# Second layer of a four-layer kernel: value products of both batches of a pair together, in one PSUM bank, every second step

## The chip, the cores and the metric

One core of a Trainium2 chip. The metric is device time in microseconds (us) of one execution of the whole program; lower is better. Engines: TensorE (PE in the profile; PEld is its weight load), VectorE (DVE), ScalarE (ACT), GpSimd (POOL) and SyncE (SP), each with its own instruction queue, in order, tied to the others by semaphores alone.

## The reference, cut to what matters

Four layers follow one another on an array of 16 batches, 128 x 256 each. The change is in the second (L1), an attention with 16 heads of 64 over 256 positions of each batch:

```python
w_heads = Wqkv @ z + Winj @ u              # one pair of weights per half of the positions
q, k, v = split(w_heads)                   # 16 heads x 64 x 256 positions each
score = einsum('bndi,bndj->bnij', q + r_w_bias, k) * SCALE
prob = softmax(score, axis=-1)
attn_vec = einsum('bnij,bndj->bndi', prob, v)
x = Wo @ attn_vec + bo + z
return (x - mean(x)) * rsqrt(var(x) + 1e-5)   # over the 128 channels
```

## The kernel before

Layer 1 works in R1 = 8 rounds of NB = 2 batches (the first and last written out, the six between them one hardware loop, function `rounds`). A round has STEPS = 16 steps: step t takes a pair of heads, t // 2, of batch b = t % 2. All work of a step is written by hand, engine by engine, in the four functions `body`; every engine runs its own list in that order and waits at semaphores.

What a step is made of, with the lines of the profile:

- scores (L1249): q times k of two heads, each on half the rows of the array, in one score bank per head. q and k are kept as a high and a low part in fp32r, three products for one. They wait for the exponentials of the step before.
- maxima of both heads (DVE, L1430), then four exponentials with their sums (ACT, L1355), a reciprocal of the sums for each head (DVE, L1436), and the normalisation in place (GpSimd, L1195).
- turn (L1261): the probabilities of step t - L_T = t - 1, transposed by TensorE into two banks; copied to pT by ACT (head 0, L1364) and DVE (head 1, L1441), `copy_turned`.
- times_v (L1277): pT times the values, step t - L_V = t - 2, into half of bank 4, each head in 64 columns of the array. `round_heads` (ACT, L1370) takes the result's high part to aT, `rest_heads` (DVE, L1446) the low part, both 256 wide; the next times_v waits for that low part (`aT_lo`), since there is one bank.
- times_wo (L1286), in even steps: output projection of the pair t - L_W = t - 4, both batches in one product of 512, summed over the round in bank 7.
- fills, after all that: one to three units from the table FILLS. A unit q, k or v is a projection of 12 products (6 for each half of its 512 columns; L1231 for q and k, L1235 for v, in the order of the table) into one of two work banks, taken by the names' position in turn; `Banks.free` makes a unit wait until the unit two before it has been read out. A q or k is read out by ACT (high part, `round_work`, L1375, L1378) and then DVE (low part, `rest_work`, L1457, L1461); a v by DVE alone (L1452). mean (L1293), var (L1300) and inv0, inv1 (L1308) are the layer normalisation of the round before: DVE centres and squares (L1487, L1489), GpSimd raises to -1/2 (`inverse_std`, L1200), DVE makes a diagonal (`make_diagonal`, L1499, in step T_DIAG), and takes the output (L1507). A name with + belongs to the next round.

At T_ZU = 13 ACT rounds the next round's inputs z and u (`round_z`, `round_u`, L1384, L1389) and DVE takes their rest (`rest_z`, `rest_u`, L1467, L1472); SP then loads the next u. These inputs are used by every projection, so round_z first waits for the last of the round:

```python
act.wait_ge(*work.full("v3b1", i - 1))     # called with i + 1
```

In DVE's body, rest_z and rest_u stand ahead of the read-out of that step's fills. The order by hand, before:

```python
L_T, L_V, L_W = 1, 2, 4
FILLS = [("q1", "k1"), ("v0b1", "q2"), ("k2",), ("v1b0", "q3"), ("k3", "v1b1"), ("q4", "mean"), ("k4",),
         ("v2b0", "q5", "var"), ("k5",), ("v2b1", "q6"), ("k6", "v3b0"), ("q7", "k7"), ("v3b1", "inv0"),
         ("inv1",), ("q0+", "k0+"), ("v0b0+",)]
T_Y, T_CENTRE, T_READ, T_DIAG, T_ZU = 2, 6, 8, 9, 13
```

PE's body: scores(t), times_v(t-2), turn(t-1), times_wo in even steps, fills. ACT's: exponentials, copy_turned, round_heads, (z, u), round_work. DVE's: maxima, copy_turned, both reciprocals, rest_heads, residual or z and u or the diagonal where due, fills.

Of the kernel before, what the change touches and what calls it, by code (L numbers as in the profile page):

```python
# [9 lines left out]
F32 = mybir.dt.float32  # L10
# [1034 lines left out]
def layer1(nc, v):  # L1045
# [10 lines left out]
    L_T, L_V, L_W = 1, 2, 4  # L1056
    SCALE = HD1 ** -0.5
    with ExitStack() as ctx:
        def sb(name, shape, dt=F32):
            return ctx.enter_context(nc.sbuf_tensor(name, shape, dt))  # L1060
# [11 lines left out]
        def place(name, shape):  # L1072

            with nc.sbuf_tensor(name + "_raw", shape, F32) as raw:
# [14 lines left out]
        pT = sb("pT", [P, 2, BANK])  # L1089
# [11 lines left out]
        pv_bank = psum[:, 4, 0:D]  # L1101
# [13 lines left out]
        FILLS = [("q1", "k1"), ("v0b1", "q2"), ("k2",), ("v1b0", "q3"), ("k3", "v1b1"), ("q4", "mean"), ("k4",),  # L1115
                 ("v2b0", "q5", "var"), ("k5",), ("v2b1", "q6"), ("k6", "v3b0"), ("q7", "k7"), ("v3b1", "inv0"),
                 ("inv1",), ("q0+", "k0+"), ("v0b0+",)]
        T_Y, T_CENTRE, T_READ, T_DIAG, T_ZU = 2, 6, 8, 9, 13
# [14 lines left out]
        pv_done = event("pv_done", STEPS)  # L1133
        aT_hi = event("aT_hi", STEPS)
        aT_lo = event("aT_lo", STEPS)
# [81 lines left out]
        def _(pe):  # L1217
# [48 lines left out]
            def times_v(i, t):  # L1266

                pair, b = divmod(t, NB)
                if t % 4 < 2:
                    pe.wait_ge(*work.out(f"v{pair // 2}b{b}", i))  # L1270
                for h in range(2):
                    pe.wait_ge(*copied[h].at(i, t))
                pe.wait_ge(*aT_lo.at(i, t - 1))
                for kt in range(2):
                    for h in range(2):
                        at = (2 * (pair % 2) + h) * HD1
                        last = mm(pv_bank[h * HD1:(h + 1) * HD1, :], vs[:, pair // 2 % 2, b, kt, at:at + HD1],  # L1277
                                  pT[:, h, kt * D:(kt + 1) * D], start=kt == 0, stop=kt == 1)
                last.then_inc(pv_done.sem, 1)

            def times_wo(i, pair):
                pe.wait_ge(*aT_lo.at(i, NB * pair + NB - 1))
# [29 lines left out]
            def body(i, first, last):  # L1312
                for t in range(STEPS):
                    scores(i, t)
                    if t >= L_V or not first:
                        times_v(i, t - L_V)
                    if t >= L_T or not first:
                        turn(i, t - L_T)
                    if first and t == L_W:
                        pe.wait_ge(wo_lo_made, 1)  # L1320
                    if t % 2 == 0 and (t >= L_W or not first):
                        times_wo(i, (t - L_W) // 2) if t >= L_W else times_wo(i - 1, (t - L_W) // 2 + PAIRS)
                    for name, r in fills(i, t, last):
# [26 lines left out]
        def _(act):  # L1350
# [10 lines left out]
            def copy_turned(i, t):  # L1361
                act.wait_ge(*turned.at(i, 2 * t))
                act.wait_ge(*pv_done.at(i, t - 1))
                nc.scalar.copy(pT[:, 0, :], turn_bank[0]).then_inc(copied[0].sem, 1)  # L1364

            def round_heads(i, t):
                pair, b = divmod(t, NB)
                act.wait_ge(*pv_done.at(i, t))
                act.wait_ge(*wo_done.at(i, pair - 2))
                nc.scalar.copy(aT[0][:, pair % 2, b, :], pv_bank).then_inc(aT_hi.sem, 1)  # L1370
# [21 lines left out]
            def body(i, first, last):  # L1392
                for t in range(STEPS):
                    exponentials(i, t, 0)
                    exponentials(i, t, 1)
                    if t >= L_T or not first:
                        copy_turned(i, t - L_T)
                    if t >= L_V or not first:
                        round_heads(i, t - L_V)
# [3 lines left out]
                    for name, r in fills(i, t, last):  # L1403
                        if name in split:
                            round_work(r, name)

            def tail(i):
                copy_turned(i - 1, STEPS - 1)
                round_heads(i - 1, STEPS - 2)
                round_heads(i - 1, STEPS - 1)  # L1410
# [16 lines left out]
        def _(dve):  # L1427
# [10 lines left out]
            def copy_turned(i, t):  # L1438
                dve.wait_ge(*turned.at(i, 2 * t + 1))
                dve.wait_ge(*pv_done.at(i, t - 1))  # L1440
                nc.vector.tensor_copy(pT[:, 1, :], turn_bank[1]).then_inc(copied[1].sem, 1)  # L1441

            def rest_heads(i, t):
                pair, b = divmod(t, NB)
                dve.wait_ge(*aT_hi.at(i, t))
                nc.vector.tensor_tensor(aT[1][:, pair % 2, b, :], pv_bank, aT[0][:, pair % 2, b, :].bitcast(F32),  # L1446
                                        ALU.subtract).then_inc(aT_lo.sem, 1)
# [61 lines left out]
            def body(i, first, last):  # L1509
                for t in range(STEPS):  # L1510
                    maxima(i, t, 0)
                    maxima(i, t, 1)
                    if t >= L_T or not first:
                        copy_turned(i, t - L_T)
                    inverse_sums(i, t, 0)
                    inverse_sums(i, t, 1)
                    if t >= L_V or not first:
                        rest_heads(i, t - L_V)
# [10 lines left out]
                    for name, r in fills(i, t, last):  # L1529
# [9 lines left out]
            def tail(i):  # L1539
                copy_turned(i - 1, STEPS - 1)  # L1540
                rest_heads(i - 1, STEPS - 2)
                rest_heads(i - 1, STEPS - 1)
# [369 lines left out]
```

## Time and profile before

| | |
|---|---|
| median of 3 runs | 1354.14 us (1354.11 to 1356.47) |
| profiled execution | 1354.62 us, its span 1352.9 us |
| TensorE busy, share of the span | 1239.4 us, 92% |
| weight load | 1005.2 us, 74% |
| VectorE | 943.3 us, 70% |
| ScalarE | 841.6 us, 62% |
| GpSimd | 502.6 us, 37% |
| mean granted TensorE clock | 0.976 of full (1.00 in the rounds of layer 1) |
| scores of layer 1, first to last | 496.5 to 1217.0 us |

A matmul's duration includes its way through the array and overlaps its neighbours, so the time a stream of products takes is the distance of their starts, not the sum of durations. The same holds for ScalarE and VectorE by a few hundredths. In timeline rows neighbouring equal instructions are merged (x8 is eight of them, with the time from the first's start to the last's end). An fp32 product is recorded as two matmuls.

### The profile page before, as it was taken

Reading aid. Unit: us, or ns where it says so; the run is one execution under the profiler, and the core shown is the slowest. Engines: PE = TensorE matmul, PEld = TensorE weight load, DVE = VectorE, ACT = ScalarE, POOL = GpSimd, SP = SyncE. Lnnn points to the kernel's source line nnn. Section 1 sums busy time; section 2 is a strip of 40 time slices with the busy share of each in tenths; the row PEclk is TensorE's granted clock in tenths of the full one; section 3 lists DMA queues with packets and bytes.
Section 4 is the critical chain, followed back from the end, with each engine's and each line's share of the span. In section 5 each row is a group of like instructions: output and inputs, shape, how many; then the busy total and the mean of one; then the engine's idle time right before and its main releaser. Section 6 shows DMA issues by size and latency. Waiting matters only on the chain. (4 is left out here: it accounts for less than half of the span.)

```text
span 1352.9 us, 31159 instructions
## 1 busy us (share of the span) xinstructions
PE 1239.4 (92%) x10866; PEld 1005.2 (74%) x10866; DVE 943.3 (70%) x1843; ACT 841.6 (62%) x2495; POOL 502.6 (37%) x490
## 2 busy tenths in 40 slices
PE   4688999999998759999999999999999999995997
PEld 3477788788776658888888888888888888882554
DVE  3688988988977366676766666667666666662554
ACT  3488988888886365555555665656556556552443
POOL 3355654654534013333333333333333333342000
PEclk8899999999999969999999999999999999997999
DMA  8000000000000020000000000000000000000100
GB/s 317 9 13 21 16 16 12 11 16 13 8 7 1 1 78 2 1 10 1 9 0 0 9 0 0 9 0 8 1 0 9 0 0 1 1 1 26 47 31 31
DMA packets 18547, 24.96 MB, mean 18 GB/s; under 512 B 1360, under 2 KB 16912, under 8 KB 18064
## 3 DMA queue, kind: packets, MB, share of 16 engines
q1 hardware_dynamic: 18448, 23.77, 5.2%
q8 instruction: 46, 0.75, 0.2%
q14 instruction: 53, 0.43, 0.1%
HBM read 21.67 MB, written 2.10 MB: 18 GB/s over the span
## 5 line engine op out<-in xcount | busy, mean ns | idle before, releaser
L1195 POOL TENSOR_TENSOR prob<-prob,l_z_inv 128x512 f32<-128x512 f32 x256 | 261.2, 1042 | 458.6 <-DVE l_z_inv L1436 458.6
L1355 ACT ACTIVATE prob<-psum,l_neg_max 128x256 f32<-128x256 f32 x512 | 236.0, 473 | 247.1 <-DVE l_neg_max L1430 232.6
L742 ACT ACTIVATE ring_e<-ring_e,neg_max 128x128 f32<-128x128 f32 x512 | 164.3, 407 | 21.3 <-DVE neg_max L911 21.2
L1430 DVE TENSOR_REDUCE l_neg_max<-psum 128x2 f32<-128x512 f32 x256 | 163.9, 681 | 10.7 <-PE psum L1249 10.7
L1261 PEld LDWEIGHTS psum<-ident,prob 128*128 128x128 f32 x1024 | 109.8, 141 | 49.0 <-issue 45.4
L1277 PE MATMUL psum<-pT,vs 128*64 128x256 f32 x1024 | 138.8, 391 | 6.7 <-DVE aTl L1446 6.5
L1261 PE MATMUL psum<-ident,prob 128*128 128x128 f32 x1024 | 139.9, 280 | 0.0
L1441 DVE COPY pT<-psum 128x512 f32<-128x512 f32 x128 | 88.1, 688 | 50.6 <-PE psum L1261 50.5
L449 POOL TENSOR_TENSOR ring_e<-ring_e,cross_add 128x512 f32<-128x512 f32 x64 | 85.3, 1350 | 90.8 <-DVE ring_e L906 90.8
L449 POOL TENSOR_TENSOR ring_e<-ring_e,self_add 128x512 f32<-128x512 f32 x64 | 86.0, 1357 | 63.1 <-DVE ring_e L906 62.4
L1446 DVE TENSOR_TENSOR aTl<-psum,aTh 128x256 fp32r<-128x256 f32 x128 | 54.4, 425 | 74.2 <-ACT aTh L1370 74.2
L1355 ACT ACTIVATION_READ_ACCUMULATOR prob<-psum,l_neg_max 128x1 f32 x512 | 103.7, 203 | 0.0
L750 ACT COPY ring_t<-psum 128x512 f32<-128x512 f32 x128 | 75.3, 588 | 45.2 <-PE psum L593 44.4
L593 PE MATMUL psum<-ident,ring_e 128*128 128x128 f32 x512 | 81.4, 283 | 15.1 <-ACT ring_t L750 14.1
L1277 PEld LDWEIGHTS psum<-pT,vs 128*64 128x64 f32 x1024 | 63.2, 136 | 43.0 <-issue 5.9
L593 PEld LDWEIGHTS psum<-ident,ring_e 128*128 128x128 f32 x512 | 61.3, 144 | 39.4 <-ACT ring_e L742 16.8
L1249 PE MATMUL psum<-kh,qh 64*128 64x256 f32 x512 | 85.9, 331 | 4.2 <-ACT prob L1355 4.2
L911 DVE TENSOR_REDUCE neg_max<-ring_e 128x4 f32<-128x512 f32 x128 | 84.8, 673 | 2.3 <-POOL ring_e L449 2.3
L1231 PE MATMUL psum<-zuh,wzh 128*128 128x256 f32 x256 | 74.6, 292 | 12.7 <-DVE zul L1472 12.7
L1364 ACT COPY pT<-psum 128x512 f32<-128x512 f32 x128 | 76.4, 597 | 2.3 <-PE psum L1261 2.3
L1231 PE MATMUL psum<-zuh,wih 128*128 128x256 f32 x256 | 72.8, 284 | 0.0
L1231 PE MATMUL psum<-zul,wih 128*128 128x256 f32 x256 | 72.7, 284 | 0.0
(198 smaller groups left out, 3200.6 us busy)
## 6 DMA issues: line engine op xcount, KB each, us to landing
wz_raw<-wz_in SPq DMA_DIRECT2D x2, 1536.0 KB, 14.6
x_in<-x SPq DMA_DIRECT2D x8, 256.0 KB, 2.9
cT<-ctxT SPq DMA_DIRECT2D x8, 256.0 KB, 2.8
w<-w_in SPq DMA_DIRECT2D x2, 1024.0 KB, 11.3
l_ub<-ctx_in SPq DMA_DIRECT2D x8, 256.0 KB, 2.7
cg<-ctx_in SPq DMA_DIRECT2D x4, 512.0 KB, 3.7
out<-fin SPq DMA_DIRECT2D x4, 512.0 KB, 2.8
wi_raw<-wi_in SPq DMA_DIRECT2D x1, 1536.0 KB, 18.0
```

The lines of the kernel that those rows point to most:

```text
L449: pool.tensor_tensor(e, e, add, ALU.add).then_inc(scores_add.sem, 1)
L593: last = nc.tensor.transpose(turn_bank[:, h * P:(h + 1) * P], ring_e[:, n % RE, h * P:(h + 1) * P], ident[:, :])
L742: last = nc.scalar.activation(e, e, ACT.Exp, bias=neg_max[:, n % RE, h:h + 1])
L911: nc.vector.tensor_reduce(neg_max[:, n % RE, :], ring_e[:, n % RE, :].rearrange("p (h k) -> p h k", h=QUAD), AX.X, ALU.max, negate=True).t ...
L1195: pool.tensor_tensor(e, e, z_inv[:, t % RE, h, :].unsqueeze(2).broadcast_to([P, 2, D]), ALU.mult)\
L1231: last = mm(o, w[wp][c][:, at:at + P], zu[xp][:, s, c, :, :].rearrange("p b l -> p (b l)"), **flags)
L1249: last = mm(score_bank[h][:, qt * D:(qt + 1) * D], q[qp][rows, pair % 2, qt, b, :], k[kp][rows, pair % 2, :, b, :], start=(qp, kp) == (0, ...
L1261: last = nc.tensor.transpose(turn_bank[h][:, kt * D + qt * P:kt * D + (qt + 1) * P], prob[:, t % RE, h, qt * D + kt * P:qt * D + (kt + 1) ...
L1277: last = mm(pv_bank[h * HD1:(h + 1) * HD1, :], vs[:, pair // 2 % 2, b, kt, at:at + HD1], pT[:, h, kt * D:(kt + 1) * D], start=kt == 0, sto ...
L1355: last = nc.scalar.activation(prob[:, t % RE, h, qt * D:(qt + 1) * D], score_bank[h][:, qt * D:(qt + 1) * D], ACT.Exp, bias=neg_max[:, t % ...
L1430: nc.vector.tensor_reduce(neg_max[:, t % RE, h, :], score_bank[h].rearrange("p (t c) -> p t c", t=2), AX.X, ALU.max, negate=True).then_inc ...
L1441: nc.vector.tensor_copy(pT[:, 1, :], turn_bank[1]).then_inc(copied[1].sem, 1)
```

## The change

The value products of both batches of a pair of heads are made in one call, every second step (L_V = 3, odd steps), into one full bank of 512 columns: sixteen records in a row. pT holds both batches. Each pair then has one round_heads and one rest_heads, 512 wide (L_R = 4, even steps: ACT at the start of the step, DVE behind the reciprocals). The semaphores pv_done, aT_hi and aT_lo count pairs. The output projection follows two steps later (L_W = 6). In even steps TensorE makes the first projection (a q) ahead of the turn and the second (a k) behind it; ACT and DVE read that q out ahead of copy_turned, and DVE's second reciprocal comes behind the copy. FILLS has two projections in each even step and one in each odd; v3b1 moves from step 12 to 13, T_ZU stays at 13.

```diff
-    L_T, L_V, L_W = 1, 2, 4
+    L_T, L_V, L_R, L_W = 1, 3, 4, 6
...
-        pT = sb("pT", [P, 2, BANK])
+        pT = sb("pT", [P, NB, 2, BANK])
...
-        pv_bank = psum[:, 4, 0:D]
+        pv_bank = psum[:, 4, :]
...
+        FILLS = [("q1", "k1"), ("v0b1",), ("q2", "k2"), ("v1b0",), ("q3", "k3"), ("v1b1",), ("q4", "k4"),
+                 ("v2b0", "mean"), ("q5", "k5"), ("v2b1",), ("q6", "var", "k6"), ("v3b0",), ("q7", "k7", "inv0"),
+                 ("v3b1", "inv1"), ("q0+", "k0+"), ("v0b0+",)]
+        T_Y, T_CENTRE, T_READ, T_DIAG, T_ZU = 5, 8, 10, 11, 13
...
+            def times_v(i, pair):
...
+                for h in range(2):
+                    pe.wait_ge(*copied[h].at(i, NB * pair + NB - 1))
+                pe.wait_ge(*aT_lo.at(i, pair - 1))
+                for b in range(NB):
+                    for kt in range(2):
+                        for h in range(2):
+                            at = (2 * (pair % 2) + h) * HD1
+                            last = mm(pv_bank[h * HD1:(h + 1) * HD1, b * D:(b + 1) * D],
+                                      vs[:, pair // 2 % 2, b, kt, at:at + HD1],
+                                      pT[:, b, h, kt * D:(kt + 1) * D], start=kt == 0, stop=kt == 1)
...
             def body(i, first, last):
                 for t in range(STEPS):
                     scores(i, t)
+                    if t % NB == L_V % NB:
+                        if t >= L_V or not first:
+                            times_v(i, (t - L_V) // NB)
+                        if t >= L_T or not first:
+                            turn(i, t - L_T)
...
+                    if t % NB == L_W % NB and (t >= L_W or not first):
+                        times_wo(i, (t - L_W) // NB) if t >= L_W else times_wo(i - 1, (t - L_W) // NB + PAIRS)
+                    now = fills(i, t, last)
+                    if not now and t % NB != L_V % NB:
+                        turn(i, t - L_T)
+                    for n, (name, r) in enumerate(now):
+                        if n == 1 and t % NB != L_V % NB and (t >= L_T or not first):
+                            turn(i, t - L_T)
...
             def tail(i):
-                times_v(i - 1, STEPS - 2)
                 turn(i - 1, STEPS - 1)
+                times_wo(i - 1, PAIRS - 3)
+                times_v(i - 1, PAIRS - 1)
                 times_wo(i - 1, PAIRS - 2)
-                times_v(i - 1, STEPS - 1)
                 times_wo(i - 1, PAIRS - 1)
...
+            def round_heads(i, pair):
+                act.wait_ge(*pv_done.at(i, pair))
                 act.wait_ge(*wo_done.at(i, pair - 2))
+                nc.scalar.copy(aT[0][:, pair % 2, :, :].rearrange("p b d -> p (b d)"), pv_bank).then_inc(aT_hi.sem, 1)
...
+                    if t % NB == L_R % NB and (t >= L_R or not first):
+                        round_heads(i, (t - L_R) // NB)
+                    now = fills(i, t, last)
                     exponentials(i, t, 0)
                     exponentials(i, t, 1)
+                    if t % NB != L_V % NB and now and now[0][0] in split:
+                        round_work(now[0][1], now[0][0])
+                        now = now[1:]
...
+                    if t % NB != L_V % NB and now:
+                        inverse_sums(i, t, 0)
+                        rest_work(now[0][1], now[0][0])
+                        now = now[1:]
+                        if t >= L_T or not first:
+                            copy_turned(i, t - L_T)
+                        inverse_sums(i, t, 1)
+                    else:
+                        if t >= L_T or not first:
+                            copy_turned(i, t - L_T)
+                        inverse_sums(i, t, 0)
+                        inverse_sums(i, t, 1)
+                    if t % NB == L_R % NB and (t >= L_R or not first):
+                        rest_heads(i, (t - L_R) // NB)
```

## Rows read from the trace of the kernel before

**Rows 1.** The variance product's line, asked in windows of the first and last round.

```profile
L1300 PE MATMUL psum<-mean_w,l_ysq x8: 250/250/271, 539.9 to 540.7; 128*128 128x1 f32 x8
...
L1300 PE MATMUL psum<-mean_w,l_ysq x8: 250/250/271, 1178.9 to 1179.7; 128*128 128x1 f32 x8
```

**Rows 2.** Waits, 905 to 996.2 us (one round): engine, line, releaser, us, times, longest.

```profile
PE psum L1277 <- DVE aTl L1446: 0.6, 2, 0.3
PE psum L1249 <- ACT prob L1355: 0.5, 2, 0.3
```

**Rows 3.** Timeline of TensorE, two steps: start us, us, engine, line, operation.

```profile
918.73 1.09 PE L1261 MATMUL psum<-ident,prob 128*128 128x128 f32 x8
...
920.36 0.28 PE L1231 MATMUL psum<-zuh,wzh 128*128 128x256 f32 x1
...
921.79 0.28 PE L1235 MATMUL psum<-wzh,zuh 128*128 128x256 f32 x1
...
923.32 0.39 PE L1249 MATMUL psum<-kh,qh 64*128 64x256 f32 x2
...
924.22 1.08 PE L1277 MATMUL psum<-pT,vs 128*64 128x256 f32 x8
925.24 1.09 PE L1261 MATMUL psum<-ident,prob 128*128 128x128 f32 x8
...
928.92 0.28 PE L1231 MATMUL psum<-zuh,wil 128*128 128x256 f32 x1
929.13 0.39 PE L1249 MATMUL psum<-kh,qh 64*128 64x256 f32 x2
```

**Rows 4.** Timeline of TensorE in windows of 0.1 us: last value products, first turn.

```profile
912.38 0.60 PE L1277 MATMUL psum<-pT,vs 128*64 128x256 f32 x4
...
912.60 0.39 PE L1277 MATMUL psum<-pT,vs 128*64 128x256 f32 x2
912.92 0.33 PE L1261 MATMUL psum<-ident,prob 128*128 128x128 f32 x1
```

**Rows 5.** Timeline of TensorE: a projection's last product, then a spread's fp32 products.

```profile
933.99 0.28 PE L1235 MATMUL psum<-wil,zuh 128*128 128x256 f32 x1
934.11 0.60 PE L1308 MATMUL psum<-l_ysq,mean_w 128*128 128x128 f32 x4
```

**Rows 6.** Timelines of ScalarE, VectorE and TensorE: a step's chain, idle time and releaser last.

```profile
924.33 1.29 DVE L1430 TENSOR_REDUCE l_neg_max<-psum 128x2 f32<-128x512 f32 x2 [0.21 <-PE psum L1249]
...
925.05 0.47 ACT L1355 ACTIVATE prob<-psum,l_neg_max 128x256 f32<-128x256 f32 x1 [2.38 <-DVE l_neg_max L1430]
...
926.87 0.59 ACT L1364 COPY pT<-psum 128x512 f32<-128x512 f32 x1
...
927.80 0.69 ACT L1375 ACTIVATE qh<-psum,cols 128x512 fp32r<-128x512 f32 x1
...
893.90 0.75 DVE L1457 SCALAR_TENSOR_TENSOR ql<-psum,cols,qh 128x512 fp32r<-128x512 f32 x1 [0.33 <-ACT qh L1375]
...
926.98 0.22 DVE L1436 RECIPROCAL l_z_inv<-l_z_sum 128x2 f32<-128x2 f32 x2
...
939.09 0.42 DVE L1446 TENSOR_TENSOR aTl<-psum,aTh 128x256 fp32r<-128x256 f32 x1 [0.57 <-ACT aTh L1370]
...
939.66 0.44 PE L1277 MATMUL psum<-pT,vs 128*64 128x256 f32 x2 [0.32 <-DVE aTl L1446]
```

**Rows 7.** Timelines of ScalarE and VectorE: rounding of the next round's inputs.

```profile
938.93 0.66 ACT L1384 CAST zuh<-xs 128x512 fp32r x1
...
939.73 1.39 DVE L1467 TENSOR_TENSOR zul<-xs,zuh 128x512 fp32r<-128x512 f32 x1 [0.21 <-ACT zuh L1384]
941.04 0.68 DVE L1472 TENSOR_TENSOR zul<-l_ub,zuh 128x512 fp32r<-128x512 f32 x1
941.65 0.41 DVE L1507 TENSOR_TENSOR xs<-l_y,psum 128x256 f32 x1
```

**Rows 8.** Timeline of ScalarE: first exponentials after the loop's jump.

```profile
953.47 0.48 ACT L1355 ACTIVATE prob<-psum,l_neg_max 128x256 f32<-128x256 f32 x1 [2.80 <-PE psum L1261]
```

More of the change, by code:

```diff
@@ L1132, in layer1 @@
         copied = [event(f"pT{h}_copied", STEPS) for h in range(2)]
-        pv_done = event("pv_done", STEPS)
-        aT_hi = event("aT_hi", STEPS)
-        aT_lo = event("aT_lo", STEPS)
+        pv_done = event("pv_done", PAIRS)
+        aT_hi = event("aT_hi", PAIRS)
+        aT_lo = event("aT_lo", PAIRS)
         wo_done = event("wo_done", PAIRS)
@@ L1264, in turn @@
                     last.then_inc(turned.sem, 1)
[L1266 to L1270, printed above, removed]
+            def times_v(i, pair):
+                if pair % 2 == 0:
+                    for b in range(NB):
+                        pe.wait_ge(*work.out(f"v{pair // 2}b{b}", i))
                 for h in range(2):
[L1272 to L1278, printed above, removed]
+                    pe.wait_ge(*copied[h].at(i, NB * pair + NB - 1))
+                pe.wait_ge(*aT_lo.at(i, pair - 1))
+                for b in range(NB):
+                    for kt in range(2):
[4 more added lines that the diff above has]
+                                      pT[:, b, h, kt * D:(kt + 1) * D], start=kt == 0, stop=kt == 1)
                 last.then_inc(pv_done.sem, 1)
             def times_wo(i, pair):
-                pe.wait_ge(*aT_lo.at(i, NB * pair + NB - 1))
+                pe.wait_ge(*aT_lo.at(i, pair))
                 if pair == 0:
@@ L1361, in copy_turned @@
             def copy_turned(i, t):
+                pair, b = divmod(t, NB)
                 act.wait_ge(*turned.at(i, 2 * t))
[L1363 to L1368, printed above, removed]
+                act.wait_ge(*pv_done.at(i, pair - 1))
+                nc.scalar.copy(pT[:, b, 0, :], turn_bank[0]).then_inc(copied[0].sem, 1)
+            def round_heads(i, pair):
+                act.wait_ge(*pv_done.at(i, pair))
                 act.wait_ge(*wo_done.at(i, pair - 2))
-                nc.scalar.copy(aT[0][:, pair % 2, b, :], pv_bank).then_inc(aT_hi.sem, 1)
+                nc.scalar.copy(aT[0][:, pair % 2, :, :].rearrange("p b d -> p (b d)"), pv_bank).then_inc(aT_hi.sem, 1)
             def round_work(i, name):
@@ L1402, in body @@
                         round_u(i + 1)
-                    for name, r in fills(i, t, last):
+                    for name, r in now:
                         if name in split:
@@ L1408, in tail @@
                 copy_turned(i - 1, STEPS - 1)
[L1409 to L1410 removed]
+                round_heads(i - 1, PAIRS - 2)
+                round_heads(i - 1, PAIRS - 1)
             round_z(0)
@@ L1438, in copy_turned, with rest_heads @@
             def copy_turned(i, t):
+                pair, b = divmod(t, NB)
                 dve.wait_ge(*turned.at(i, 2 * t + 1))
[L1440 to L1447, printed above, removed]
+                dve.wait_ge(*pv_done.at(i, pair - 1))
+                nc.vector.tensor_copy(pT[:, b, 1, :], turn_bank[1]).then_inc(copied[1].sem, 1)
+            def rest_heads(i, pair):
+                dve.wait_ge(*aT_hi.at(i, pair))
+                hi, lo = (w[:, pair % 2, :, :].rearrange("p b d -> p (b d)") for w in aT)
+                nc.vector.tensor_tensor(lo, pv_bank, hi.bitcast(F32), ALU.subtract).then_inc(aT_lo.sem, 1)
             def rest_work(i, name):
@@ L1510, in body @@
                 for t in range(STEPS):
+                    now = fills(i, t, last)
                     maxima(i, t, 0)
                     maxima(i, t, 1)
[L1513 to L1518, printed above, removed]
+                    if t % NB != L_V % NB and now:
[12 more added lines that the diff above has]
+                        rest_heads(i, (t - L_R) // NB)
                     if t == T_Y:
@@ L1528, in body @@
                         make_diagonal(i)
-                    for name, r in fills(i, t, last):
+                    for name, r in now:
                         if is_made(name):
```

17 lines of the change are left out of this document (2 added, 15 removed).

## The prediction

> **What bounds the kernel now.** I read the page's busy shares first (TensorE 92%), then windows over the second layer. That layer is eight rounds of 16 steps; the variance product comes once a round and starts at 539.9 us in the first and at 1178.9 in the last, seven periods of 91.3 us, 5.7 a step [rows 1]. In one period TensorE waits for something the profile names for only 0.6 + 0.5 us [rows 2]. So TensorE issues nearly without a gap, and what a step costs is the sum of its products' start-to-start times; VectorE, ScalarE and GpSimd have slack. Two consequences: anything taken out of TensorE's stream is gained in full, and a new wait in it is lost in full.
>
> A step with two projections [rows 3]: scores 0.90 us (923.32 to 924.22), values of one batch 1.02, then 3.89 to the next scores. Of that a projection is 1.43 (920.36 to 921.79); the change from a full-array product back to scores on half the rows is 0.10 (928.92 to 929.13, 0.21 for the ordinary 0.12); so the turn is 3.89 - 2.86 - 0.10 = 0.93, and the output projection 1.63 - 0.93 = 0.70. A pair of steps holds two of each, one output projection and three value, query or key projections: 2 x (0.90 + 1.02 + 0.93 + 0.10) + 0.70 + 3 x 1.43 = 10.89; eight pairs make 87.1 of the 91.3, the rest is mean, variance, two spreads and the waits.
>
> **What the change does to TensorE's own stream.** The value products come in concurrent pairs 0.22 apart, but the turn starts 0.32 after the last pair (912.60 to 912.92) [rows 4]: 0.10 is the change of array shape. Both batches (sixteen records, eight concurrent pairs) are then 1.02 + 4 x 0.215 = 1.88 once instead of 2.04, saving 0.16 a pair. The even step now goes from scores straight to the output projection. The trace has no such place; bounds are 0.12 between starts (no change of shape) and 0.32 (values to turn); I take 0.21, as from scores to values, so scores stay at 0.90. A projection ahead of the turn costs nothing: a full-array fp32 product starts 0.12 after the last fp32r one, the ordinary distance [rows 5]. Even step: 0.90 + 0.70 + 1.43 + 0.93 + 1.43 + 0.10 = 5.49. Odd step: 0.90 + 1.88 + 0.93 + 1.43 + 0.10 = 5.24. Together 10.73 for 10.89: 0.16 x 8 = 1.28 us a round. The new table of fills also ends the steps without a projection, which are those that wait for the exponentials: with that, all of [rows 2] goes away, 1.1. Removed: 2.38 a round.
>
> **What it adds: waits.** On VectorE the even step's order is now maxima, one reciprocal, rest of q, copy of the turned half, the other reciprocal, and only then the rest of the heads (aT low), 512 wide. The value products in the very next step wait for that low part, since both batches share one bank and it can't be refilled before. Before, that wait looked one step back too, but nothing of a projection stood ahead of it. The chain from the start of the even step's scores [rows 6]: maxima at 1.01; exponentials 0.72 later, 1.73; four of them take 1.82 (925.05 to 926.87), so q's high part starts at 3.55 (projection is done at 3.03 + 0.2) and takes 0.69 + 0.04; rest of q 0.75, which lets the next start 0.08 early, 0.67; copy 0.61; reciprocal 0.11; rest of heads 0.68, taken from the subtraction of that width in [rows 7]; 0.15 to TensorE (939.09 + 0.42 to 939.66). Sum 6.48. TensorE would be there at 5.49 + 0.90 = 6.39. An ordinary pair waits 0.09; four do, 0.36 a round. The copies on ScalarE and the normalisation on GpSimd have half a microsecond or more of cover: the turn comes 2.8 us and more after the step's start. SP's load of the next round's u waits for the rest of u, which is later by some microseconds, and has a whole round to land; GpSimd's inverse deviation moves from step 8 to 10 and is wanted in step 11. Both cost nothing.
>
> Where VectorE has other work at the end of an odd step, the maxima start later and the wait grows. Step 7 holds the mean: centring and squaring, two operations of 0.68 starting when the mean is done, put the maxima 0.43 later: wait 0.52 in step 9. In step 10 the key projection takes the bank of q, because the variance stands between; q is read out at 4.28 + 0.75 + 0.1 = 5.12, and TensorE is there at 0.90 + 0.70 + 1.43 + 0.93 + 0.9 (eight small products 0.1 apart [rows 1] and the change) = 4.86: 0.27. Step 11 has the diagonal, and step 12 a spread product that makes TensorE later too; I set the one against the other.
>
> **The turn of the round** is the largest term. v3b1 moves from step 12 to step 13, while the rounding of the next round's inputs (T_ZU) stays at 13, and round_z waits for v3b1's bank to be full. Before, that wait was long over. Now, counted from the end E of that projection [rows 7]: z's high part at E + 0.20 (as maxima after scores, 0.32 after the last start); rest of z 0.80 later, E + 1.00; rest of u 1.31 later, 2.31; the copy that frees the bank at 2.92 (0.61), done 3.61; TensorE 3.76. It wanted that bank for the next round's q at 0.53 (spread, change) + 0.90 + 0.70 = 2.13. **Wait 1.63.** Queued behind the rest of z and u on VectorE are also the output (0.41, [rows 7]) and step 14's maxima, at E + 3.86; by the chain above values of step 15 may start at 3.86 + 5.47 = 9.33, TensorE is there at 3.76 + 1.43 + 0.93 + 1.43 + 0.10 + 0.90 = 8.55: 0.8 more.
>
> One more term stands at the loop's end: ScalarE idles 2.80 us ahead of the first exponentials of a round, and the row names a turn as releaser [rows 8]; I hold it for the loop's jump, since turns end often and only five such gaps exist (one for each jump back). ScalarE's last copy now ends about 1.2 before the new round's scores, so rounding the heads starts 1.6 after it and the exponentials 0.3 late: 0.3 more wait in step 1. The Trainium skill, "Runtime: NRT & Kernel Launch", Instruction fetch mechanics, says that a taken branch out of the fetched pages forces a fetch before execution goes on; by that the gap stays, by the releaser that the row names it would vanish and the sum be 2.1 us less in seven rounds. No row of this trace tells them apart.
>
> **Sum.** New waits of a round: 0.36 + 0.3 + 0.52 + 0.27 + 1.63 + 0.8 = 3.88; less 2.38 removed: +1.50, times the seven rounds that have a successor: +10.5. The last has no turn of the round: about -0.5. The tail ends on one chain, with 0.86 more of values and 0.2 on each of the two wider head operations: +1.3. Total +11.3 on the profiled execution's 1354.6; that stands 0.5 above the median, so 1365.4 against 1354.1. Layers 0, 2 and 3 don't change.
>
> **Rivals.** (1) The gain on paper: no new wait shows, every product moves up. -2.38 x 8 + 1.3 = -18: 1336. For it: the ordinary pair is short by only 0.09, within my error. Against: the 1.63 is a plain order of instructions, not a fine balance. Chance 0.13. (2) Only the turn of the round and step 9 cost, the chain being some 0.3 quicker than summed: waits 1.63 + 0.5 + 0.2, what is removed, and with tail and last round 1355. Chance 0.17. This is also the case in which the merged products cost as much as they save, since a change of shape stands at both ends of every unit. (3) The chain to the low part of the heads is dearer: 0.5 us more (a later copy, VectorE held up in front of the maxima) comes in seven steps of each round, 3.5 x 8 = 28 more: 1393. It decides as soon as the chain exceeds 6.5; its lower end is a few tenths. Chance 0.12. The forecast has 0.58.
>
> **How the numbers follow.** A measurement here tells 0.2% (2.7 us) from nothing. Slower: forecast, rival 3 and a little of rival 2: 0.71. Same: 0.10, faster: rival 1 and a third of rival 2, 0.19. The range leaves out rival 1 and most of rival 3: 1350 to 1378. Its lower end is rival 2 with 0.3 a round less, its upper end the forecast with 0.2 more on seven waits a round. The forecast alone would be 1357 to 1374.
>
> **What would show it.** In the changed kernel: period between variance products near 92.8 for 91.3; value products (L1277's successor) released by the low part of the heads some five to seven times a round, about 0.1 mostly and 0.5 to 0.8 after the mean and at step 15; the first projection of step 14 idle 1.6 before it, named for the read-out of v3b1; scores no longer waiting for exponentials; 1.9 us for the sixteen value records; DVE's rest of z starting a microsecond after v3b1, TensorE's clock still full. Wrong if the period is 91 or less, or if no gap stands ahead of the next round's q.

## Result: 1.03% slower

The changed kernel takes 1368.71 us (median of 4 runs, 1367.83 to 1370.38) against 1354.64 for the one before (4 runs): ratio 1.0103, 95% interval 1.0085 to 1.0120. Forecast were 1365.4 and a range of 1350 to 1378. The profiled execution took 1370.38 us for the 1354.62 of before, 15.8 more.

The page first: instructions fell by 258, of which 64 each on ScalarE and VectorE are the second round_heads and rest_heads of each pair; the rest isn't counted as busy. TensorE has the same 10866 matmuls and a lower share.

```profile
span 1368.7 us, 30901 instructions
PE 1244.3 (91%) x10866; PEld 1018.9 (74%) x10866; DVE 928.4 (68%) x1779; ACT 835.2 (61%) x2431; POOL 506.0 (37%) x490
```

The variance product, asked in windows of the first and the last round, as in [rows 1]:

```profile
L1303 PE MATMUL psum<-mean_w,l_ysq x8: 169/250/250, 554.7 to 555.4; 128*128 128x1 f32 x8
...
L1303 PE MATMUL psum<-mean_w,l_ysq x8: 169/250/250, 1203.8 to 1204.5; 128*128 128x1 f32 x8
```

(1203.8 - 554.7) / 7 = 92.73 us for 91.29: 1.44 a round, 10.1 in seven. (That the product comes three steps later in its round doesn't touch the period.) Of the other 5.7, 1.2 lie ahead of the layer's rounds (first scores 497.7 for 496.5), 2.4 between the last scores and the third layer's first product (1228.7 to 1259.0 against 1216.8 to 1244.7), 0.5 in the first and last round, and 1.5 behind the third layer's first product, where the code is the same.

An ordinary pair of steps on TensorE, and the end of VectorE's chain in it. Columns as in [rows 3]:

```profile
975.50 0.39 PE L1250 MATMUL psum<-kh,qh 64*128 64x256 f32 x2
976.41 1.95 PE L1279 MATMUL psum<-pT,vs 128*64 128x256 f32 x16
978.28 1.09 PE L1262 MATMUL psum<-ident,prob 128*128 128x128 f32 x8
...
980.74 0.39 PE L1250 MATMUL psum<-kh,qh 64*128 64x256 f32 x2
981.65 0.50 PE L1289 MATMUL psum<-aTh,woh 128*128 128x512 f32 x1
982.44 0.28 PE L1232 MATMUL psum<-zuh,wzh 128*128 128x256 f32 x1
983.88 1.04 PE L1262 MATMUL psum<-ident,prob 128*128 128x128 f32 x8
...
986.27 0.39 PE L1250 MATMUL psum<-kh,qh 64*128 64x256 f32 x2
987.18 1.08 PE L1279 MATMUL psum<-pT,vs 128*64 128x256 f32 x8
```

```profile
986.36 0.67 DVE L1460 TENSOR_TENSOR aTl<-psum,aTh 128x512 fp32r<-128x512 f32 x1
```

Both batches' values take 1.87 us (976.41 to 978.28), forecast 1.88. The pair takes 986.27 - 975.50 = 10.77 for 10.89 before, which is 0.96 a round. The low part of the heads is ready at 987.03, the value products start 0.15 later, at 987.18, which is also 0.91 after their scores, the ordinary distance: chain and stream end at the same moment.

What TensorE waits for in one round (925.5 to 1018.3 us; columns as in [rows 2]):

```profile
PEld psum L1232 <- DVE zul L1485: 1.6, 1, 1.6
PE psum L1232 <- DVE vs L1465: 1.2, 1, 1.2
...
PE psum L1311 <- DVE ql L1470: 0.9, 1, 0.9
PE psum L1279 <- DVE aTl L1460: 0.8, 2, 0.5
...
PEld psum L1232 <- DVE ql L1470: 0.2, 1, 0.2
```

Five waits are new: the first projection of the next round (L1232, for the bank of v3b1), the spread product of step 12 (L1311, for q7's bank), two of the values for the low part, and k6 for the bank of q6. Measured by the distance of starts, less that of an undisturbed place, they are 1.48, 1.19, 0.61 (step 15), 0.33 (step 9) and 0.19: 3.80 a round. The waits of [rows 2] in the old places are gone.

By the same measure [rows 2] understates what the kernel before waited. From scores to scores its steps 13, 14, 15 and 0 take 3.72, 6.89, 4.72 and 6.81 us (starts 934.64, 938.36, 945.25, 949.97, 956.78), and without a wait they would take 3.39, 6.51, 4.38 and 6.50: steps of two projections and an output projection take 6.51 and 6.50 elsewhere (steps 10 and 4), steps of one projection 4.38 in e5, and in step 13 a spread product of 0.44 replaces its 1.43. That is 1.36 of waiting; with 0.3 ahead of the variance product (0.33 from the last product to it instead of 0.12, and 0.1 in its own products) the kernel before waited some 1.7 a round, where the view names 1.1.

So the period closes: 3.80 of new waits, plus 0.2 for the variance, which now stands between the two projections of step 10 and costs 1.0 there (6.72 - 5.53 - 0.19) against 0.80 at the end of a step (e8), less 0.96 of stream and 1.7 of old waits, is 1.3 to 1.4 for the measured 1.44.

The second of the new waits I hadn't expected. TensorE, VectorE and GpSimd around step 12:

```profile
932.98 2.44 DVE L1512 TENSOR_SCALAR l_ysq<-ident,l_rstd 128x128 f32<-128x128 f32 x4
...
933.08 2.06 POOL L1196 TENSOR_TENSOR prob<-prob,l_z_inv 128x512 f32<-128x512 f32 x2 [3.77 <-DVE l_z_inv L1449]
...
933.47 0.39 PE L1250 MATMUL psum<-kh,qh 64*128 64x256 f32 x2
...
935.94 0.67 DVE L1443 TENSOR_REDUCE l_neg_max<-psum 128x2 f32<-128x512 f32 x1
...
939.20 0.75 DVE L1470 SCALAR_TENSOR_TENSOR ql<-psum,cols,qh 128x512 fp32r<-128x512 f32 x1 [1.33 <-ACT qh L1384]
...
940.00 0.71 PE L1311 MATMUL psum<-l_ysq,mean_w 128*128 128x128 f32 x4 [0.93 <-DVE ql L1470]
```

The four small operations of the diagonal take 2.44 us while GpSimd normalises (933.08 to 935.14): the first and last 0.27 and 0.28, the two between 1.06 and 1.08. So the maxima start 2.47 after their scores instead of 1.01, every link behind them is 1.46 late, and q7 is read out at 939.95; the spread product has its bank and starts at 940.00.

The turn of the round, on ScalarE, VectorE and TensorE:

```profile
946.09 0.62 ACT L1393 CAST zuh<-xs 128x512 fp32r x1 [0.92 <-PE psum L1236]
...
946.87 1.22 DVE L1480 TENSOR_TENSOR zul<-xs,zuh 128x512 fp32r<-128x512 f32 x1 [1.39 <-ACT zuh L1393]
...
948.00 0.68 DVE L1485 TENSOR_TENSOR zul<-l_ub,zuh 128x512 fp32r<-128x512 f32 x1
948.61 0.68 DVE L1465 COPY vs<-psum 128x512 f32<-128x512 f32 x1
949.21 0.41 DVE L1520 TENSOR_TENSOR xs<-l_y,psum 128x256 f32 x1
...
949.42 0.38 PE L1232 MATMUL psum<-zuh,wzh 128*128 128x256 f32 x1 [1.22 <-DVE vs L1465]
...
954.86 0.44 PE L1279 MATMUL psum<-pT,vs 128*64 128x256 f32 x2 [0.54 <-DVE aTl L1460]
```

This is the forecast's chain, link by link: v3b1's last product, z's high part, rest of z, rest of u, copy, first projection. Rest of z takes nearly twice as long as rest of u, of the same size. GpSimd normalises beside it:

```profile
945.49 2.04 POOL L1196 TENSOR_TENSOR prob<-prob,l_z_inv 128x512 f32<-128x512 f32 x2 [3.75 <-DVE l_z_inv L1449]
```

In the kernel before it was so too (GpSimd from 938.54 for 2.04, rest of z 1.39 in [rows 7]); with GpSimd idle, in e6, rest of z takes 0.68. So some 0.5 of the 1.48 at the turn of the round is the overlap of the two engines, as in step 12. That share is read from durations; no run changes it alone.

### The profile page after: what moved, and what is told of

Same layout as the page of the kernel before. It is cut to its first block and busy times, and to the rows that moved or that the text cites. A ratio compares the mean times of both kernels' runs of the same rounds, so it can differ in the third digit from the quotient of the medians.

```text
span 1368.7 us, 30901 instructions
## 1 busy us (share of the span) xinstructions
PE 1244.3 (91%) x10866; PEld 1018.9 (74%) x10866; DVE 928.4 (68%) x1779; ACT 835.2 (61%) x2431; POOL 506.0 (37%) x490
## 5 line engine op out<-in xcount | busy, mean ns | idle before, releaser
L1196 POOL TENSOR_TENSOR prob<-prob,l_z_inv 128x512 f32<-128x512 f32 x256 | 264.2, 1043 | 465.4 <-DVE l_z_inv L1449 465.4
L1262 PEld LDWEIGHTS psum<-ident,prob 128*128 128x128 f32 x1024 | 113.1, 141 | 27.6 <-issue 24.2
L1279 PE MATMUL psum<-pT,vs 128*64 128x256 f32 x1024 | 124.6, 385 | 7.1 <-DVE aTl L1460 7.0
L1470 DVE SCALAR_TENSOR_TENSOR ql<-psum,cols,qh 128x512 fp32r<-128x512 f32 x64 | 48.1, 751 | 83.1 <-ACT qh L1384 83.1
L1279 PEld LDWEIGHTS psum<-pT,vs 128*64 128x64 f32 x1024 | 69.1, 136 | 44.0 <-DVE aTl L1460 7.3
L1232 PE MATMUL psum<-zuh,wzh 128*128 128x256 f32 x256 | 79.3, 310 | 20.6 <-DVE zul L1485 11.3
L1232 PE MATMUL psum<-zuh,wzl 128*128 128x256 f32 x256 | 73.1, 285 | 0.0
L1232 PE MATMUL psum<-zuh,wih 128*128 128x256 f32 x256 | 73.0, 285 | 0.0
```

The costliest lines, as they stand in the source:

```text
L1196: pool.tensor_tensor(e, e, z_inv[:, t % RE, h, :].unsqueeze(2).broadcast_to([P, 2, D]), ALU.mult)\
L1232: last = mm(o, w[wp][c][:, at:at + P], zu[xp][:, s, c, :, :].rearrange("p b l -> p (b l)"), **flags)
L1262: last = nc.tensor.transpose(turn_bank[h][:, kt * D + qt * P:kt * D + (qt + 1) * P], prob[:, t % RE, h, qt * D + kt * P:qt * D + (kt + 1) ...
L1279: last = mm(pv_bank[h * HD1:(h + 1) * HD1, b * D:(b + 1) * D], vs[:, pair // 2 % 2, b, kt, at:at + HD1], pT[:, b, h, kt * D:(kt + 1) * D], ...
```

## Experiments

Times are compared by the ratio to the kernel before on the same chip (its median there 1355.4 to 1356.1 us); the changed kernel has 1.0103. The period is that of the variance product, as above.

| kernel | ratio (95% interval) | period, us |
|---|---|---|
| before | 1 | 91.29 |
| the change | 1.0103 (1.0085 to 1.0120) | 92.73 |
| e5: new table alone | 1.0104 (1.0088 to 1.0119) | 92.76 |
| e9: merged values alone | 0.9978 (0.9969 to 0.9987) | 90.71 |
| e4: change, turn first | 1.0067 (1.0053 to 1.0081) | 92.01 |
| e1: change, diagonal earlier | 1.0027 (1.0017 to 1.0037) | 91.54 |
| e2: change, v3b1 read first | 1.0059 (1.0045 to 1.0073) | 92.13 |
| e6: e1 and both other places | 0.9946 (0.9933 to 0.9959) | 89.89 |
| e7: e6, centring moved | 0.9928 (0.9915 to 0.9941) | 89.64 |
| e8: e7, turn first | 0.9892 (0.9878 to 0.9907) | 88.90 |
| e10: e8, other tail | 0.9883 (0.9864 to 0.9902) | 88.90 |

### e1: the diagonal in VectorE's idle time

```diff
@@ VectorE's body, odd steps
+                        if t == T_DIAG:
+                            make_diagonal(i)
                         if t >= L_T or not first:
                             copy_turned(i, t - L_T)
...
-                    if t == T_DIAG:
-                        make_diagonal(i)
```

> The changed kernel with VectorE's diagonal of step 11 moved ahead of that step's copy of the turned half. Theory (the 0.93 us that the spread product of step 12 waits for q7's read-out comes from maxima that are 1.46 late, behind a diagonal that takes 2.44 us because GpSimd normalises at the same time): in the idle 1.4 us ahead of the copy, with GpSimd idle, it takes about 1.1 us, the maxima of step 12 start at their usual 1.0 after the scores, the wait goes to 0 to 0.1 and the period from 92.73 to 91.8 to 91.9; 8 rounds, 6.5 to 7.5 us less than the changed kernel, about 1362. Rival (the wait is q's own chain, behind the exponentials): period unchanged, 92.7, time 1368 to 1369.

Measured: period 91.54, 1.19 less, time 1359.12. On VectorE and TensorE:

```profile
925.86 0.87 DVE L1512 TENSOR_SCALAR l_ysq<-ident,l_rstd 128x128 f32<-128x128 f32 x4
...
934.00 0.60 PE L1311 MATMUL psum<-l_ysq,mean_w 128*128 128x128 f32 x4
```

The same four operations take 0.87 us with GpSimd idle, the spread product follows its projection at once, and the round gets shorter by all of the 1.19, over a quarter more than the 0.93 that the profile names as the wait and from which 91.8 to 91.9 was expected: the distance between starts was the better measure. The rival falls. The time fell by 0.76%, some 10 us; eight times 1.19 is 9.5, and the intervals don't tell the two apart.

### e2: v3b1 read out ahead of the rest of z and u

```diff
@@ VectorE's body
+                    if t == T_ZU:
+                        rest_work(now[0][1], now[0][0])
+                        now = now[1:]
                     if t == T_ZU and not last:
                         rest_z(i + 1)
                         rest_u(i + 1)
```

> The changed kernel with v3b1's bank read out by VectorE ahead of the rest of z and u in step 13. Theory (the first projection of the next round waits for the order rest of z, rest of u, copy): the copy fits while VectorE waits for z's high part, the low parts are done 0.6 us sooner, the wait of 1.4 shrinks to 0.8, the one at step 15 stays 0.6, period 92.1, seven rounds: 4 us less than the changed kernel, about 1364.5. Rival (that wait is made up again at step 15 or elsewhere): less than 1 us off the time.

Measured: 92.13, exactly 0.6 less. The first projection now waits 0.5 and the named releaser is the rest of u (the low parts), no longer the copy; the values of step 15 still wait (0.9 named for steps 9 and 15 together, 0.8 in the change). So the order of VectorE's work at the turn of the round is a cause: with the copy (0.61) moved ahead in it, the period is 0.60 shorter.

### e4: the projection ahead of the turn undone

```diff
@@ TensorE's body, even steps
-                    if not now and t % NB != L_V % NB:
-                        turn(i, t - L_T)
-                    for n, (name, r) in enumerate(now):
-                        if n == 1 and t % NB != L_V % NB and (t >= L_T or not first):
-                            turn(i, t - L_T)
+                    if t % NB != L_V % NB and (t >= L_T or not first):
+                        turn(i, t - L_T)
+                    for n, (name, r) in enumerate(now):
@@ ScalarE and VectorE: copy_turned and both reciprocals ahead of q, as in odd steps
```

> The changed kernel with the projection ahead of the turn undone: in even steps TensorE turns first and then makes both projections, ScalarE and VectorE copy the turned half first, and the low part of the heads stands ahead of the rest of q on VectorE. Theory (that move bought no time by itself and its price is the chain through the rest of q): no wait of the value products for the low part is left (0.33 in step 9 and 0.61 in step 15 go), but q is read out about 0.6 later, so the spread product of step 12 and the key projection of step 10 wait 0.5 to 0.6 longer each: period 92.7 to 93.1, time 1368 to 1371. Rival (the move is what makes the merged products possible): the turn waits for GpSimd's normalisation by 0.3 or more in each even step, period 95 and more, time above 1385.

Measured: 92.01, 0.72 less than the change, where I expected up to 0.4 more. Waits of TensorE, same window:

```profile
PE psum L1311 <- DVE ql L1465: 1.4, 1, 1.4
...
PE psum L1232 <- DVE ql L1465: 0.8, 1, 0.8
...
PE psum L1232 <- DVE vs L1460: 0.3, 1, 0.3
```

The waits for q's bank grew as expected (0.9 to 1.4 and 0.2 to 0.8), those of the values are gone, and so is most of the one at the turn of the round (1.2 to 0.3). That last I had missed: the turn, 0.93 us long, now stands between the scores and the next round's q, and covers it. The rival falls too: no turn waits for GpSimd in this view. The projection ahead of the turn costs 0.72 a round here, half of the loss.

### e5: the table of fills alone

```diff
@@ the kernel before
-        FILLS = [("q1", "k1"), ("v0b1", "q2"), ("k2",), ...
-        T_Y, T_CENTRE, T_READ, T_DIAG, T_ZU = 2, 6, 8, 9, 13
+        FILLS = [("q1", "k1"), ("v0b1",), ("q2", "k2"), ...
+        T_Y, T_CENTRE, T_READ, T_DIAG, T_ZU = 2, 8, 10, 11, 13
```

> The kernel before with the new table of fills and the due steps that go with it (T_CENTRE, T_READ, T_DIAG as in the change; the residual stays in step 2, as the output projection needs it there); value products still made for each batch. Theory (the table takes away the short steps that wait for exponentials, and in the old order values, turn and output projection, 2.65 us, stand between the scores and the next round's q, so the late v3b1 costs nothing): the 1.1 us of waits go, up to 1 us comes back at the banks of q6 and q7; period 90.2 to 91.1, time 1345 to 1353. Rival (v3b1 in the step of T_ZU costs its 1.4 us in any order): period 91.6 and more, time 1357 and above.

Measured: 92.76 and 1.0104, as slow as the whole change. I had forecast a gain. The numbers are in the rival's range, but its mechanism isn't what happened. Waits in a round, and the timeline of TensorE at step 14:

```profile
PE psum L1308 <- DVE ql L1457: 0.9, 1, 0.9
...
PE psum L1231 <- DVE ql L1457: 0.8, 1, 0.8
```

```profile
947.12 0.47 PE L1286 MATMUL psum<-aTh,woh 128*128 128x512 f32 x1
947.89 0.28 PE L1231 MATMUL psum<-zuh,wzh 128*128 128x256 f32 x1
```

The next round's q comes right behind the output projection, 0.77 us, with no wait: that part of the theory holds, the late v3b1 is free in this order. The loss is at the banks of q7 and q6: the table puts a third unit (inv0, var) into a step of two projections, and the third takes the bank of the first, which ScalarE and VectorE read out one after the other. At q7 the diagonal has a part in it again:

```profile
932.05 1.49 DVE L1499 TENSOR_SCALAR l_ysq<-ident,l_rstd 128x128 f32<-128x128 f32 x4
```

It and a copy of values behind it start the maxima of step 12 at 934.06, 2.75 after their scores (931.31) instead of 1.01. No run takes the diagonal out of e5, so the split of that wait between the third unit and the diagonal isn't shown.

### e9: the merged value products alone

The form of e4 with the old table:

```diff
@@ e4
-        FILLS = [("q1", "k1"), ("v0b1",), ("q2", "k2"), ...
-        T_Y, T_CENTRE, T_READ, T_DIAG, T_ZU = 5, 8, 10, 11, 13
+        FILLS = [("q1", "k1"), ("v0b1", "q2"), ("k2",), ...
+        T_Y, T_CENTRE, T_READ, T_DIAG, T_ZU = 5, 6, 8, 9, 13
```

> The merged value products alone: turn first in every step, the old table of fills and its due steps (but the residual in step 5, behind the later output projection). Theory (merging takes 0.16 us a pair out of TensorE's stream, and the wait for the low part of the heads is not on the path where no projection stands ahead of it): 1.3 us a round from the stream and 0.3 to 1.1 of the waits in steps 13 to 15; period 89.4 to 90.3 for 91.3, time 1341 to 1350. Rival (merging itself costs, since each change of array shape is only moved): period 91.3 or more, 1354 and above.

Measured: 90.71, 0.58 less than before, time 0.22% less; the expected 89.4 to 90.3 was too much. Merging is a gain, and the rival falls; but waits of about the old size stay, at other places: 0.7 of the turn in step 14 for GpSimd and 0.3 of the mean for y are named, 1.21 and 0.61 by the distance of starts. Of the turn's wait, 0.45 is a normalisation that takes 1.49 us instead of 1.04 while VectorE works beside it:

```profile
934.89 1.55 DVE L1475 TENSOR_TENSOR zul<-xs,zuh 128x512 fp32r<-128x512 f32 x1
...
934.85 2.49 POOL L1196 TENSOR_TENSOR prob<-prob,l_z_inv 128x512 f32<-128x512 f32 x2 [3.73 <-DVE l_z_inv L1444]
```

VectorE's operation is longer too, 1.55 for the 0.68 that it takes with GpSimd idle (e6).

The parts nearly add up: merging -0.58, the table +1.47, together +0.89 where e4 shows +0.72; the projection ahead of the turn +0.72 makes +1.44.

### e6 and e7: the same work in places where VectorE is idle

```diff
@@ the change
-                 ... ("v3b0",), ("q7", "k7", "inv0"), ("v3b1", "inv1"), ...
+                 ... ("v3b0", "v3b1"), ("q7", "k7"), ("inv0", "inv1"), ...
@@ round_z
-                    act.wait_ge(*work.full("v3b1", i - 1))
+                    act.wait_ge(*work.full("k7", i - 1))
@@ ScalarE: round_z, round_u ahead of step 13's exponentials
@@ VectorE, odd steps: make_diagonal, or rest_z and rest_u, ahead of copy_turned
@@ e7 also, VectorE in step 8, between the first reciprocal and the rest of q
+                        if t == T_CENTRE:
+                            centre(i, "mean")
```

> The changed kernel with v3b1 in step 11, the two spread products together in step 13, z and u rounded for the next round at the start of step 13 (behind k7, now the last user of the old ones) and their rest, like the diagonal, ahead of the copy of the turned half on VectorE. Theory (the loss sits in places where VectorE's extra work stands at the end of an odd step and where a third unit of a step waits for q's bank, not in the merged products): the waits of steps 12 (0.93), 14 (1.4) and 15 (0.6) go, those of step 9 (0.3) and 10 (0.1) stay; period 92.73 to 89.8, time 1346 to 1350, faster than before. Rival (VectorE has no room left and the work only delays the next copy or the next maxima): period 91 and more, 1356 and above.

> As e6_both_in_gaps, and VectorE centres and squares in step 8, in its idle time ahead of the rest of q, instead of at the end of step 7. Theory: the value products of step 9 no longer wait 0.3 us, so the period falls from 89.8 to 89.5 and the time by 2 to 3 us, to 1344 to 1347. Rival (the two operations of 0.7 don't fit and push the rest of q): the same time as e6_both_in_gaps or more.

Measured: 89.89 and 89.64, 1348.71 and 1345.23 us. Both as expected; the waits at steps 12 and 14 are gone, and centring in step 8 takes another quarter of a microsecond a round. Nothing in the merged products had to be undone for that. The wait of the values for the low part that is left in e7 (0.4) stands in step 1, behind the loop's jump on ScalarE:

```profile
944.94 0.59 ACT L1379 CAST aTh<-psum 128x512 fp32r<-128x512 f32 x1 [2.57 <-issue]
945.42 0.48 ACT L1364 ACTIVATE prob<-psum,l_neg_max 128x256 f32<-128x256 f32 x1
```

Step 0's scores start at 943.15, so its exponentials come 2.27 after them instead of 1.73. The first and the last period, with no jump in them, are 89.27 and 89.37 us, those between 89.71 to 89.94 us.

### e8: and the turn first

The edit of e4 on e7, with the variance in step 9 (T_READ too).

> As e7_centre_too, with the turn ahead of both projections in even steps, as in e4_turn_first, and the variance in step 9. Theory (the projection ahead of the turn is only one way of keeping the units behind q off q's bank; with no unit there it buys nothing): no wait left, period 89.3 to 89.6, the same time as e7_centre_too within 2 us. Rival (the turn then waits for the normalisation in every even step): 0.1 to 0.4 more in eight steps, period 90.2 to 92.5, 1350 and above.

Measured: 88.90, 1340.71 us: 0.74 a round better than e7, not the same. Waits of TensorE in a round, all that the view lists:

```profile
PEld psum L1262 <- issue: 3.1, 8, 0.4
PEld psum L1250 <- issue: 0.8, 1, 0.8
PEld psum L1262 <- POOL prob L1196: 0.2, 1, 0.2
```

Only weight loads wait: eight times some 0.4 ahead of a turn and once 0.8 ahead of scores, both as in the change and for nothing that the profile names, and once 0.2 for GpSimd. From scores to scores, against a round of e7 inside the loop, e8 gains 0.45 in step 1 (5.24 for 5.69) and 0.52 in steps 9 and 10 (11.59 for 12.11), and loses 0.17 in step 14, where that turn waits. Of the 0.52, 0.16 is a wait of the values in step 9; the rest comes of moving the variance, 0.19 of it k6's wait for q6. So the projection ahead of the turn isn't neutral where no unit stands behind q's bank: its longer chain to the low part costs some 0.6 of the 0.74 here. The rest belongs to the variance, since the edit moved both. This version beats both kernels: 1.1% less than before.

### e10: the tail

```diff
-                turn(i - 1, STEPS - 1)
                 times_wo(i - 1, PAIRS - 3)
+                turn(i - 1, STEPS - 1)
```

> As e8_turn_first_gaps, with the output projection of pair 5 ahead of the last turn, outside the loop. Theory (in the tail TensorE stands idle for 2 us ahead of the last turn, waiting for GpSimd, while a projection of 0.8 us that is ready comes behind it; the idle time also lowers the granted clock there): from the last scores to the first product of the third layer 31.6 us become 30.5 to 30.9, up to 29.5 if the clock holds; the period stays 88.9, the time within 2 us of e8_turn_first_gaps. Rival (the value products behind the turn wait for the copies anyway and the projection fills no time there): 31.4 to 31.8, unchanged.

Measured: 31.7 us from the last scores (1199.4) to the third layer (1231.1), against 31.5 to 31.6 in e8: the rival holds. Two rows of it, TensorE, and a stretch with the granted clock (after the engines' busy times):

```profile
1207.87 3.68 PE L1279 MATMUL psum<-pT,vs 128*64 128x256 f32 x16 [1.47 <-DVE aTl L1455]
```

```profile
1206.00:1210.00 4.00, 2.53 (x14) 1.53 (x14) 1.29 (x2) 0.51 (x2) 0.00 (x0) 0.57 0.00 0
```

The projection fills 0.8 of the idle time ahead of the turn, and the idle time appears again behind it, 1.47 ahead of the values. They wait for the low part of the pair before them, which VectorE makes behind its copy of the last turn (1206.44 and 1207.04, done at 1207.72). The mean clock is then 0.57, near the lower of its two levels (1.2 GHz), and the sixteen value records take 3.68 us for the 1.95 of the loop. In e8 they take 2.75 in a stretch with 0.60, so the two tails differ in where the clock fell too; what the order alone is worth stays open.

## Why the prediction was right, and where it wasn't

**TensorE's stream.** 10.77 a pair for 10.73. The value products are as forecast; the output projection behind the scores takes 0.79 (981.65 to 982.44) where I had carried over 0.70, the change of shape showing in its first product. Saved 0.96 a round, not 1.28.

**The ordinary wait** of 0.09: not there. TensorE's 0.1 more and a chain that ends at 6.44 for my 6.48 (whose terms add up to 6.50) meet exactly. That the pair came out within 0.05 of my 10.82 is luck: 0.09 too little in the stream, 0.09 too much in the wait.

**Step 9, step 10:** 0.33 for 0.52, 0.19 for 0.27. **The turn of the round:** 1.48 for 1.63, and 0.61 for 0.8 in step 15; rest of z took 1.13 to the next start instead of 1.31, both times with GpSimd at work beside it. e2 shows the order to be a cause.

**The loop's jump:** forecast 0.3 in step 1, measured nothing on TensorE in the change. The gap itself is real and moved. ScalarE at the end of a round:

```profile
957.85 0.60 ACT L1374 COPY pT<-psum 128x512 f32<-128x512 f32 x1
...
960.34 0.59 ACT L1379 CAST aTh<-psum 128x512 fp32r<-128x512 f32 x1 [1.90 <-issue]
```

In [rows 8] it was 2.80 us and named a turn. Now another instruction is the first of the loop's body, the gap stands ahead of that one, 1.90 long, and nothing is named. That agrees with the rule of "Runtime: NRT & Kernel Launch" (Instruction fetch mechanics) in the Trainium skill, and not with the releaser of the row. In the kernel before, the program does make those exponentials wait for a turn, but for the one of two steps earlier, which started at 947.18, over six microseconds ahead of them. The last copy ends 0.74 before the new round's scores (958.45, 959.19) where I had put 1.2, but the gap is 1.90 and not 2.80, so the exponentials at 961.01 come 1.82 after the scores, 0.09 late. In e7 the gap is 2.57 long, and there the wait that I had forecast shows, 0.45 in step 1: the mechanism was right, its size depends on how long the gap is.

**Step 12** is the step of the prediction that failed: "I set the one against the other." That was no working. It left out that the spread product takes the bank of q7, and it gave the diagonal no length. In the kernel before, the diagonal takes 1.48 us (from 916.12), with GpSimd done at 916.93; here it takes 2.44, with GpSimd at work through nearly all of it. It cost 1.19 a round (e1), nearly a third of all new waits. It was made up by the ordinary wait, the jump and four terms each 0.1 to 0.2 too high: 3.80 for 3.88 in sum. On the other side stand 0.96 for 1.28 of stream and some 1.7 for 1.1 of old waits, which I had taken from what the view names, and 0.2 for the variance that I hadn't counted. The period, 92.73 for "near 92.8", is closer than its terms deserve: errors of up to 1.2 in both directions cancelled, which is luck.

**The tail:** 2.4 us for 1.3. I counted widths alone. TensorE waits for the last normalisation there, and its granted clock falls; the mean over 1232 to 1236 us is 0.75 (the figure behind the engines' busy times):

```profile
1234.08 1.11 PE L1262 MATMUL psum<-ident,prob 128*128 128x128 f32 x4 [1.97 <-POOL prob L1196]
```

```profile
1232.00:1236.00 4.00, 2.03 (x10) 1.64 (x10) 0.82 (x3) 1.13 (x3) 2.04 (x2) 0.75 0.00 0
```

Before, the values of step 14 stood in that time, and the clock was 1.00 from 1217 to 1229 us, though they waited 1.66 for the low part there. How the 1.1 more splits between the order and the clock isn't shown. Of the 15.8 us between the profiled executions, seven periods are 10.1 (forecast 10.5) and the tail 2.4 (1.3); the first and last round, forecast at -0.5, are +0.5, and 2.7 lie outside the layer's rounds and tail, where nothing was forecast.

**The rivals.** The gain on paper didn't come, but it was there to be had: e8's period is 2.4 less than before, what rival 1 counted (though of other parts), by other places for VectorE's work, the variance moved and the turn first. Rival 2's condition, a chain short enough that an ordinary pair doesn't wait, held; its time of 1355 didn't, since step 12 and the others cost more than the turn of the round and step 9 alone. Rival 3's dearer chain didn't appear.

## What to carry over

When a stream-bound engine has its work regrouped, list for each unit which buffer it takes and who frees it, and count the chain that frees it: here the regrouped products were a small gain (0.58 a round), the places of VectorE's diagonal, rounding and centring and of the units in the table cost 3.1 (the change against e7), and a projection ahead of the turn some 0.6 to 0.7. Extra work of a helper engine belongs into its idle time (and, since VectorE and GpSimd slow each other here, into that of the other one too) ahead of something that is late anyway, not at the end of a step, where the next step's first link waits for it. A term that is "set against another" without a sum is the one to work out. And the waits that the profile names were all shorter here than what they cost: take the distance of starts against an undisturbed place, for the old waits too.

## What the runs showed of the hardware

- VectorE's 128x128 fp32 multiply of SBUF data by a column takes 0.28 us alone, 0.87 for four (e1), and 2.44 for four while GpSimd's 128x512 multiplies run; single ones last up to 1.08 us, about one of GpSimd's operations (1.04). Its 128x512 subtraction of two SBUF tensors takes 0.68 us with GpSimd idle (e6) and 1.22 to 1.55 beside it (the change, e9). The Trainium skill ("SBUF — State Buffer", SBUF: two separate sides) describes a port pair that the two engines share, locked for a whole instruction; the traces agree.
- A change of array shape costs 0.1 us at the scores' and at the values' side (0.21 between starts for 0.12, 0.32 for 0.22); at the output projection behind the scores another 0.1 shows in its first product (0.79 us for 0.70 behind a turn).
- The jump back of a hardware loop cost ScalarE 1.7 us of idle time on average in e1, 1.8 in the change and 2.9 in the kernel before (3.2 at most), which the profile puts down to nothing, or to a wait that had long ended.
- In the tail, waits of 1.28 us (e10) to 1.97 (the change, e8) ahead of the last turn, with more behind it, were followed by stretches of 4 us with a mean granted clock of 0.57 to 0.82. In the kernel before, a wait of 1.66 between the last two turns was not, and waits of up to 1.5 us inside the loop left it at 1.00.
